# Graph attention on one Trainium2 core: the weighted sum over neighbours with the features as the loaded operand

## The chip, the cores and the metric

One core of a Trainium2 chip runs the whole program. The metric is the device time of one execution in microseconds; three runs of the kernel before were timed.

## The reference, cut to what matters

Four graphs of 256 nodes go through two graph attention layers (8 heads of 32 outputs) and then through a transformer block with a mixture of experts. The change touches the graph layers alone:

```python
def gat_layer(x, adj, W, a_self, a_neigh, b):
    feat = jnp.einsum('nf,hfo->hno', x, W)
    attn_self = jnp.einsum('hno,ho->hn', feat, a_self)
    attn_neigh = jnp.einsum('hno,ho->hn', feat, a_neigh)
    e = attn_self[:, :, None] + attn_neigh[:, None, :]
    e = jax.nn.leaky_relu(e, LRELU_ALPHA)
    e = e + MASK_VAL * (1.0 - adj)[None, :, :]
    alpha = jax.nn.softmax(e, axis=-1)
    out = jnp.einsum('hnm,hmo->hno', alpha, feat) + b[:, None, :]
    out = jnp.transpose(out, (1, 0, 2)).reshape(out.shape[1], -1)
    return jax.nn.elu(out)
...
x = x + _L0_xattn_ref(ctx_512, _layernorm(x, axis=-1), ...)
x = x + _L0_ffn_ref(_layernorm(x, axis=-1), ...)
```

## The kernel before, in words

Each engine runs its own hand-written program; semaphores join them. The work of one graph is cut into 48 steps, and tables of steps (`UNIT_AT`, `TRANS_LAG`, `PV_LAG`, `OUT_AT`, `QKV_AT`, ...) say which piece stands in which step. First the graph layers of graph 0 run alone (the part ahead of the loop). Then a loop of three passes runs, in each step, the graph layers of graph b + 1 (`gat(b + 1, s)`) and behind them the pieces of the transformer block of graph b. Last comes the block of graph 3 alone. On every engine the order within a step is fixed: the graph layer's instructions first, then the block's.

A graph layer has 8 units: two halves of the rows (t = 0, 1, 128 rows each) times four pairs of heads. For a unit, TensorE makes the scores of two heads (`zb`, L424), ScalarE copies them (L625), VectorE does the leaky ReLU and the mask (L895, L904), GpSimd shifts (L735), TensorE transposes four 128x128 blocks into the bank `tb` (L432), ScalarE takes the exponential of that bank into `gpT` (L630), and TensorE multiplies with the features (L443). The transposes of unit k stand 4 steps behind its scores, the product 5 steps: so in one step TensorE transposes unit k + 1 and then multiplies unit k.

The product of a unit is 4 calls. A call loads a 128x128 block of the attention weights and streams 33 columns of `feat`: the 32 features of a head and a column of ones, so that the sum of the weights, by which the result is divided, comes out as column 33. The result stands in `ob` with the rows of the graph on the partitions. After the four units of a half, in the step `done(l, t)`, VectorE divides (L911, L913) and adds the bias (L916); one step later (`ELU_LAG`) ScalarE (L634) and VectorE (L920, L921) do the ELU. In step `OUT_AT` (20) TensorE transposes layer 0's output (L455), which starts layer 1. `ob`, `tb` and `zb` are single banks: the next writer waits until the last reader is through (`o_free`, `t_free`, `z_free`).

Of the kernel before, what the change touches and what calls it, by code (L numbers as in the profile page):

```python
# [12 lines left out]
P = 128  # L13
# [5 lines left out]
FE = FO + 1  # L19
# [63 lines left out]
ELU_LAG = 1  # L83
# [56 lines left out]

def summed(s):

    return [n for n, at in enumerate(SUM_AT) if at == s]
# [17 lines left out]
def block_program(nc, x, ctxT, w0, w1, gat_rows, norm_cols, qk_rows, wqkv, wo, wgate, wgu, wd, consts, spread, out):  # L161
    ctx = ExitStack()
    with ctx:
        def sb(name, shape, dt=F32):
            return ctx.enter_context(nc.sbuf_tensor(name, shape, dt))
# [4 lines left out]
        def sem(name):  # L170
            return ctx.enter_context(nc.semaphore(name))
# [11 lines left out]
        qkw = sb("qkw", [P, 2 * HD])  # L183
# [27 lines left out]
        gsum = sb("gsum", [P, H])  # L211
        go = rows[:, 2 * D:4 * D].rearrange("p (t d) -> p t d", t=T)
# [3 lines left out]
        hid = sb("hid", [P, T, D])  # L216
        hn = gex
# [64 lines left out]
        pv_done, o_free = sem("pv_done"), sem("o_free")  # L282
        gout_ready, gexp_ready, gres_ready, hn_ready = sem("gout_ready"), sem("gexp_ready"), sem("gres_ready"), sem("hn_ready")
# [18 lines left out]
        def t_value(b, l, n):  # L302


            return b * 2 * (NU + 3) + l * (NU + 3) + n + 1
# [39 lines left out]
        def _(sp):  # L345
# [9 lines left out]
            sp.dma_start(qkw[:, :], qk_rows).then_inc(in_gat, 16)  # L355
# [30 lines left out]
        def _(pe):  # L386
            def gat(b, a):

                for l in range(2):
# [45 lines left out]
                    for k in units(l, a - PV_LAG):  # L435
                        t, hp = divmod(k, H // 2)
                        pe.wait_ge(t_free, t_value(b, l, k + 2) + 1)
                        if hp == 0:
                            pe.wait_ge(o_free, b * 2 * T + l * T + t + 1)
                        for h in range(2):  # L440
                            hh = 2 * hp + h
                            for m in range(T):
                                mm = pe.matmul(ob[:, hh * FE:(hh + 1) * FE], gpT[:, k % 3, h, m, :], feat[:, m, hh, :],  # L443
                                               start=(m == 0), stop=(m == T - 1))
                        mm.then_inc(pv_done, 1)
                if a in (OUT_AT, HN_AT):
# [161 lines left out]
        def _(act):  # L608
            def gat(b, a):
                for l in range(2):  # L610
# [20 lines left out]
                    for t in range(T):  # L631
                        if a == done(l, t) + ELU_LAG:
                            act.wait_ge(gout_ready, b * 2 * T + l * T + t + 1)
                            act.activation(gex[:, t, :], go[:, t, :], ACT.Exp).then_inc(gexp_ready, 1)  # L634
# [181 lines left out]
        def _(dve):  # L816
# [37 lines left out]
            def gat(b, a):  # L854
# [18 lines left out]
                for l in range(2):  # L873
# [33 lines left out]
                    for t in range(T):  # L907
                        if a == done(l, t):
                            dve.wait_ge(pv_done, unit(b, l, 4 * t + 4))
                            o_ = ob[:, 0:H * FE].rearrange("p (h o) -> p h o", h=H)  # L910
# [3 lines left out]
                               .then_inc(o_free, 1)  # L914
                            dve.wait_ge(o_free, b * 2 * T + l * T + t + 2)
# [241 lines left out]
            for t in range(T):  # L1157
                link(dve.memset(feat[:, t, :, FO:FE], 1.0))

            dve.sem_inc(z_free, 1)  # L1160
            dve.sem_inc(t_free, 1)
            dve.sem_inc(o_free, 1)
# [73 lines left out]
```

## Time and profile before

| | |
|---|---|
| median of 3 timed runs | 677.07 us (676.18 to 681.5) |
| span of the profiled execution | 676.1 us |
| TensorE matmul busy | 604.8 us, 89% of the span |
| TensorE weight load busy | 445.9 us, 66% |
| VectorE busy | 441.0 us, 65% |
| ScalarE busy | 266.7 us, 39% |
| GpSimd busy | 292.0 us, 43% |
| mean granted TensorE clock | 0.944 |

The profile gives each instruction's start and duration on the chip. A matmul's duration holds its way through the array, so the pace of matmuls is read from start to start. PE is TensorE's matmul, PEld its weight load, DVE is VectorE, ACT is ScalarE, POOL is GpSimd. The granted clock is 1.00 at the full level and 0.50 at the lower. The part ahead of the loop ends near 100 us, the passes of the loop end near 250, 403 and 557 us, and the last block fills the rest.

### The profile page before, as it was taken

Reading aid. Unit: us, or ns where it says so; the run is one execution under the profiler, and the core shown is the slowest. Engines: PE = TensorE matmul, PEld = TensorE weight load, DVE = VectorE, ACT = ScalarE, POOL = GpSimd, SP = SyncE. Lnnn points to the kernel's source line nnn. Section 1 sums busy time; section 2 is a strip of 40 time slices with the busy share of each in tenths; the row PEclk is TensorE's granted clock in tenths of the full one; section 3 lists DMA queues with packets and bytes.
Section 4 is the critical chain, followed back from the end, with each engine's and each line's share of the span. In section 5 each row is a group of like instructions: output and inputs, shape, how many; then the busy total and the mean of one; then the engine's idle time right before and its main releaser. Section 6 shows DMA issues by size and latency. Waiting matters only on the chain.

```text
span 676.1 us, 11574 instructions
## 1 busy us (share of the span) xinstructions
PE 604.8 (89%) x3140; PEld 445.9 (66%) x3140; DVE 441.0 (65%) x1277; ACT 266.7 (39%) x653; POOL 292.0 (43%) x588
## 2 busy tenths in 40 slices
PE   2786938979999998879999998879999998999998
PEld 1573933559678873558778973458777974676786
DVE  5727537975738756985738765986738766565363
ACT  2313305546533304636633304647633303674020
POOL 1514325885424023886425023886424126773000
PEclk9997558898999998979999998989999999999999
DMA  8900000000000000000000000000000000000000
GB/s 313 380 6 0 2 16 4 1 2 1 0 1 2 2 26 10 4 0 2 0 1 1 1 26 10 1 0 1 1 1 1 1 1 16 1 1 1 1 1 16
DMA packets 8305, 14.51 MB, mean 21 GB/s; under 512 B 860, under 2 KB 7068, under 8 KB 7988
## 3 DMA queue, kind: packets, MB, share of 16 engines
q1 hardware_dynamic: 8244, 13.76, 5.8%
q8 instruction: 31, 0.51, 0.3%
q14 instruction: 30, 0.25, 0.1%
HBM read 12.70 MB, written 1.05 MB: 20 GB/s over the span
## 4 chain that ended last, share of the span: by engine, by line
PE 56%; DVE 16%; issue 13%; POOL 9%; ACT 4%; POOLq 1%; DMA 1%; DVEq 0%; ACTq 0%; SPq 0%
PE bank L565 10%; PE bank L463 9%; PE ob L443 9%; PE bank L523 5%; PE tb L432 5%; PE bank L542 4%; DVE tt L904 3%; POOL m L775 2%; PE bank L538 2%; PE bank L534 2%; PE bank L509 2%; DVE lr L895 2%; PE zb L424 1%; ACT prob L666 1%; PE zb L414 1%
## 5 line engine op out<-in xcount | busy, mean ns | idle before, releaser
L735 POOL TENSOR_SCALAR tt<-tt,gmn 128x256 f32<-128x256 f32 x128 | 77.1, 613 | 64.1 <-DVE gmn L904 63.5
L509 PE MATMUL bank<-wqkv_sb,hT 128*128 128x512 f32 x192 | 97.9, 648 | 0.0
L666 ACT ACTIVATE prob<-bank,sneg,rms 128x128 f32<-128x128 f32 (+1 forms) x128 | 64.0, 507 | 68.5 <-DVE sneg L995 67.7
L775 POOL TENSOR_TENSOR m<-early,rope_s 128x256 f32<-128x256 f32 x80 | 70.8, 908 | 42.1 <-ACT early L647 41.8
L463 PE MATMUL bank<-m,wgu_sb 128*128 128x128 f32 (+1 forms) x480 | 86.6, 330 | 1.0 <-DVE m L1025 0.6
L791 POOL TENSOR_SCALAR prob<-prob,srcp 128x128 f32<-128x128 f32 (+1 forms) x128 | 53.7, 436 | 55.5 <-DVE srcp L1066 55.4
L463 PEld LDWEIGHTS bank<-m,wgu_sb 128*128 128x128 f32 x480 | 71.2, 191 | 9.2 <-issue 2.2
L443 PEld LDWEIGHTS ob<-feat,gpT 128*128 128x128 f32 x512 | 75.8, 227 | 0.8 <-issue 0.6
L443 PE MATMUL ob<-feat,gpT 128*128 128x33 f32 x512 | 75.2, 297 | 0.0
L895 DVE SCALAR_TENSOR_TENSOR lr<-zs 128x512 f32<-128x512 f32 x64 | 50.9, 797 | 25.3 <-ACT zs L625 22.6
L904 DVE CUSTOM_DVE_ANT_0 tt<-lr,maskv 128x256 f32<-128x256 f32 x128 | 62.3, 522 | 3.5 <-issue 2.9
L523 PE MATMUL bank<-kT,qT 128*128 128x128 f32 (+1 forms) x256 | 62.3, 360 | 0.9 <-ACT prob L666 0.9
L625 ACT ACTIVATE zs<-zb 128x512 f32<-128x512 f32 x64 | 38.3, 599 | 59.7 <-PE zb L424 56.5
L509 PEld LDWEIGHTS bank<-wqkv_sb,hT 128*128 128x128 f32 x192 | 36.3, 203 | 38.0 <-issue 35.0
L565 PE MATMUL bank<-wo_sb,qT 128*128 128x256 f32 x256 | 59.7, 383 | 0.3 <-ACT qT L672 0.3
L647 ACT ACTIVATE early<-bank 128x512 f32<-128x512 f32 x40 | 24.1, 603 | 89.8 <-PE bank L509 89.8
L565 PEld LDWEIGHTS bank<-wo_sb,qT 128*128 128x128 f32 x256 | 47.3, 190 | 10.0 <-issue 4.5
L432 PE MATMUL tb<-cst,tt 128*128 128x128 f32 x256 | 48.8, 322 | 4.6 <-ACT gpT L630 3.8
L523 PEld LDWEIGHTS bank<-kT,qT 128*128 128x128 f32 x256 | 41.4, 199 | 12.4 <-issue 6.3
L994 DVE TENSOR_REDUCE smx<-bank 128x2 f32<-128x512 f32 (+1 forms) x48 | 33.0, 686 | 24.8 <-PE bank L525 21.8
L630 ACT ACTIVATE gpT<-tb 128x512 f32<-128x512 f32 x64 | 38.4, 599 | 20.4 <-PE tb L432 19.9
L432 PEld LDWEIGHTS tb<-cst,tt 128*128 128x128 f32 x256 | 34.5, 169 | 17.1 <-issue 7.6
(151 smaller groups left out, 1026.5 us busy)
## 6 DMA issues: line engine op xcount, KB each, us to landing
wqkv_sb<-wqkv_dram SPq DMA_DIRECT2D x1, 3072.0 KB, 12.4
wgu_sb<-wgu_dram SPq DMA_DIRECT2D x2, 1408.0 KB, 11.2
wo_sb<-wo_dram SPq DMA_DIRECT2D x1, 2048.0 KB, 17.8
wd_sb<-wd_dram SPq DMA_DIRECT2D x1, 1408.0 KB, 15.6
xin<-x_dram SPq DMA_DIRECT2D x4, 256.0 KB, 2.7
out_dram<-rows SPq DMA_DIRECT2D x8, 128.0 KB, 1.9
rows<-gat_rows_dram SPq DMA_DIRECT2D x1, 512.0 KB
cst<-consts_dram SPq DMA_DIRECT2D x1, 425.0 KB, 3.6
```

What stands on the lines that cost most here:

```text
L432: mm = pe.transpose(tb[:, (h * T + m) * P:(h * T + m + 1) * P], tt[:, k % 3, h, m * P:(m + 1) * P], ident)
L443: mm = pe.matmul(ob[:, hh * FE:(hh + 1) * FE], gpT[:, k % 3, h, m, :], feat[:, m, hh, :], start=(m == 0), stop=(m == T - 1))
L463: mm = pe.matmul(ps[:, m * N + c0:m * N + c1], wgu_sb[:, m, k, n * P:(n + 1) * P], tokT[:, k, c0:c1], start=(k == 0), stop=(k == KT - 1))
L509: mm = pe.matmul(ps[:, :], hT[:, k, t * P:(t + 1) * P], wqkv_sb[:, k, c * G * HD:(c + 1) * G * HD], start=(k == 0), stop=(k == KT - 1))
L523: pe.matmul(ps[:, i * nk:(i + 1) * nk], qT[:, G * g + h, t * P:(t + 1) * P], kT[:, g, 0:nk], start=True, stop=False)
L565: mm = pe.matmul(bank_of(w)[:, 0:D], lhs[:, k, t * P:(t + 1) * P], rhs[:, k, :], start=(k == 0), stop=(k == end - 1))
L666: ins = act.activation(prob[:, n % 5, i * nk:(i + 1) * nk], ps[:, i * nk:(i + 1) * nk], ACT.Exp, bias=sneg[:, n, i:i + 1], scale=rq(g, t, ...
L735: ins = pool.tensor_scalar(tt[:, k % 3, h, :], tt[:, k % 3, h, :], -1.0, gmn[:, k % 3, h:h + 1], ALU.mult, ALU.add)
L775: ins = pool.tensor_tensor(dst[:, :, c, :], src[:, :, 1 - c, :], s_, ALU.mult)
L791: ins = pool.tensor_scalar(part_, part_, srcp[:, n, i:i + 1], 1.0, ALU.mult, ALU.mult)
L895: dve.scalar_tensor_tensor(lr[:, k % 2, :], zs[:, k % 2, :], 0.2, zs[:, k % 2, :], ALU.mult, ALU.min)\
L904: ins = dve.tensor_tensor_reduce(tt[:, k % 3, h, :], lr[:, k % 2, h * N:(h + 1) * N], maskv[:, t, :], 1.0, 3e38, ALU.add, ALU.min, gmn[:, ...
```

## The change

The two operands of the product change places. `feat` gets 64 columns per head (32 features, a column of ones, 31 zeros); the 64 columns of one head are the loaded operand, and a 128x128 block of the transposed attention weights streams, 128 columns. The two heads of a unit go to the two column halves of the array: head 0 writes partitions 0 to 63 of `ob`, head 1 partitions 64 to 127. So the result stands turned: head and feature on the partitions, rows of the graph on the columns. When a half of the rows is done, ScalarE copies `ob` to the new tensor `goT`; one step later TensorE turns it back with four transposes into `tb`, and VectorE divides from there. The ELU moves one step on. The order in which `tb` is filled is now a computed list (`TURNED`). To make room, `qkw` lies in the memory of `hid`.

```diff
-FE = FO + 1
+FE = 2 * FO
...
-ELU_LAG = 1
+BACK_LAG, ELU_LAG = 1, 2
...
+def turned_fills():
+    order = []
+    for a in range(STEPS):
+        for l in range(2):
+            if a == TERMS_AT[l]:
+                order.append((l, 0))
+            if a == PARTS_AT[l]:
+                order.append((l, 1))
+            order += [(l, k + 2) for k in units(l, a - TRANS_LAG)]
+            order += [(l, "back", t) for t in range(T) if a == done(l, t) + BACK_LAG]
+        if a in (OUT_AT, HN_AT):
+            order.append((0 if a != HN_AT else 1, NU + 2))
+    return {fill: n for n, fill in enumerate(order)}
...
+        goT = sb("goT", [P, H // 2, P])
+        qkw = hid[:, 0, :]
...
                         pe.wait_ge(t_free, t_value(b, l, k + 2) + 1)
-                        if hp == 0:
-                            pe.wait_ge(o_free, b * 2 * T + l * T + t + 1)
-                        for h in range(2):
-                            hh = 2 * hp + h
-                            for m in range(T):
-                                mm = pe.matmul(ob[:, hh * FE:(hh + 1) * FE], gpT[:, k % 3, h, m, :], feat[:, m, hh, :],
-                                               start=(m == 0), stop=(m == T - 1))
+                        if hp == 0 and (t or l or not isinstance(b, int)):
+                            pe.wait_ge(goT_ready, b * 2 * T + l * T + t)
+                        for m in range(T):
+                            for h in range(2):
+                                mm = pe.matmul(ob[h * FE:(h + 1) * FE, hp * P:(hp + 1) * P], feat[:, m, 2 * hp + h, :],
+                                               gpT[:, k % 3, h, m, :], start=(m == 0), stop=(m == T - 1))
                         mm.then_inc(pv_done, 1)
+                    for t in range(T):
+                        if a == done(l, t) + BACK_LAG:
+                            pe.wait_ge(goT_ready, b * 2 * T + l * T + t + 1)
+                            pe.wait_ge(t_free, back_value(b, l, t))
+                            pe.nop(nofuse=True)
+                            for hp in range(H // 2):
+                                mm = pe.transpose(tb[:, hp * P:(hp + 1) * P], goT[:, hp, :], ident)
+                            mm.then_inc(t_full, 1)
...
+                        if a == done(l, t):
+                            act.wait_ge(pv_done, unit(b, l, 4 * t + 4))
+                            if t or l or not isinstance(b, int):
+                                act.wait_ge(gout_ready, b * 2 * T + l * T + t)
+                            act.activation(goT[:, :, :].rearrange("p h q -> p (h q)"), ob[:, :], ACT.Copy).then_inc(goT_ready, 1)
...
-                        if a == done(l, t):
-                            dve.wait_ge(pv_done, unit(b, l, 4 * t + 4))
-                            o_ = ob[:, 0:H * FE].rearrange("p (h o) -> p h o", h=H)
+                        if a == done(l, t) + BACK_LAG:
+                            dve.wait_ge(t_full, back_value(b, l, t))
+                            o_ = tb[:, :].rearrange("p (h o) -> p h o", h=H)
                             link_a(b, dve.reciprocal(gsum[:, :], o_[:, :, FO]))
...
-                link(dve.memset(feat[:, t, :, FO:FE], 1.0))
+                link(dve.memset(feat[:, t, :, FO:FE], 0.0))
+                link(dve.memset(feat[:, t, :, FO:FO + 1], 1.0))
```

Line numbers shift with it: L432 becomes L456, L443 becomes L466, and the transposes back are L475; ScalarE's copy is L667; VectorE's division L947 and L949.

On TensorE in the loop, layer 0, the step behind the first half's last product. Before, the four transposes of a unit into `tb`, the product of the unit before it into `ob`, and then the block's own transposes of `m`:

```order
L432 MATMUL tb<-cst,tt 128x128 x4
L439 REGISTER_ALU
L443 MATMUL ob<-feat,gpT 128x33 x4
L477 REGISTER_ALU
L517 MATMUL bank<-cst,m 128x128
L518 MATMUL bank<-cst,m 128x128
```

Of the change, with the transposes back of `goT` into the same bank:

```order
L456 MATMUL tb<-cst,tt 128x128 x4
L463 REGISTER_ALU
L466 MATMUL ob<-gpT,feat 64x128 x4
L472 REGISTER_ALU
L475 MATMUL tb<-cst,goT 128x128 x4
L508 REGISTER_ALU
L548 MATMUL bank<-cst,m 128x128
L549 MATMUL bank<-cst,m 128x128
```

The four transposes back stand between the product and the block's work, and write the bank that the unit's transposes of the same step have just filled; the exponential has to empty it first.

On ScalarE at the same place: the exponentials of two units (`gpT`), between them the block's copy (`qT`) and four softmax rows (`prob`). Before:

```order
L630 ACTIVATE gpT<-tb 128x512
L319 REGISTER_ALU
L656 ACTIVATE qT<-bank 128x4x128
L662 REGISTER_ALU
L666 ACTIVATE prob,ssum<-bank,sneg,rms 128x128 x4
L627 REGISTER_ALU
L630 ACTIVATE gpT<-tb 128x512
```

Of the change:

```order
L661 ACTIVATE gpT<-tb 128x512
L666 REGISTER_ALU
L667 ACTIVATE goT<-ob 128x512
L343 REGISTER_ALU
L692 ACTIVATE qT<-bank 128x4x128
L698 REGISTER_ALU
L702 ACTIVATE prob,ssum<-bank,sneg,rms 128x128 x4
L658 REGISTER_ALU
L661 ACTIVATE gpT<-tb 128x512
```

The copy of `ob` has come in behind the first exponential; the second, which empties `tb` for the transposes back, stays behind the softmax rows.

On TensorE ahead of the loop, the last units of layer 0 and the transposes of the layer's output (`gex`). Before:

```order
L432 MATMUL tb<-cst,tt 128x128 x4
L443 MATMUL ob<-feat,gpT 128x33 x4
L432 MATMUL tb<-cst,tt 128x128 x4
L443 MATMUL ob<-feat,gpT 128x33 x8
L455 MATMUL tb<-cst,gex 128x128 x4
```

Of the change:

```order
L475 MATMUL tb<-cst,goT 128x128 x4
L456 MATMUL tb<-cst,tt 128x128 x4
L466 MATMUL ob<-gpT,feat 64x128 x4
L456 MATMUL tb<-cst,tt 128x128 x4
L466 MATMUL ob<-gpT,feat 64x128 x8
L475 MATMUL tb<-cst,goT 128x128 x4
L486 MATMUL tb<-cst,gex 128x128 x4
```

Both turns stand alone between the layer's own instructions here; no block work lies beside them.

## Rows read from the trace of the kernel before

**Rows 1.** The page's head: the span.

```profile
span 676.1 us, 11574 instructions
```

**Rows 2.** The page's costliest groups, the product: records | busy us, mean ns | idle before.

```profile
L443 PE MATMUL ob<-feat,gpT 128*128 128x33 f32 x512 | 75.2, 297 | 0.0
```

**Rows 3.** Stretches: us, busy us (records) of PE, PEld, DVE, ACT, POOL, granted clock, DMA.

```profile
64.00:90.00 26.00, 22.94 (x100) 20.18 (x100) 13.78 (x45) 8.17 (x15) 10.02 (x16) 0.50 0.01 2
...
294.00:298.00 4.00, 0.06 (x1) 0.09 (x2) 1.63 (x2) 4.00 (x13) 4.00 (x6) 0.76 0.00 0
298.00:304.00 6.00, 6.00 (x28) 4.59 (x29) 5.86 (x13) 1.86 (x4) 4.89 (x9) 0.59 0.00 0
304.00:325.00 21.00, 20.65 (x155) 17.40 (x155) 13.15 (x41) 15.17 (x48) 12.72 (x33) 1.00 0.01 2
```

**Rows 4.** TensorE in order of time, layer 1 in the loop: start us, us, instruction.

```profile
371.28 0.98 PE L443 MATMUL ob<-feat,gpT 128*128 128x33 f32 x8
372.10 1.14 PE L463 MATMUL bank<-m,wgu_sb 128*128 128x128 f32 x8
373.07 0.60 PE L432 MATMUL tb<-cst,tt 128*128 128x128 f32 x4
373.51 0.98 PE L443 MATMUL ob<-feat,gpT 128*128 128x33 f32 x8
```

**Rows 5.** TensorE in order of time, around smaller array shapes.

```profile
281.95 0.27 PE L518 MATMUL bank<-cst,m 128*128 128x128 f32 x1
282.16 0.39 PE L424 MATMUL zb<-pair_r,pair_l 48*128 48x512 bf16 x1
282.47 0.66 PE L432 MATMUL tb<-cst,tt 128*128 128x128 f32 x4
...
315.37 0.22 PE L525 MATMUL bank<-causal,identb 128*128 128x128 bf16 x1
315.42 0.65 PE L523 MATMUL bank<-kT,qT 128*128 128x256 f32 x2
...
339.25 0.29 PE L408 MATMUL tb<-identb,parts 128*48 128x128 bf16 x2
339.47 1.99 PE L414 MATMUL zb<-w1x,hT 128*128 128x256 f32 x8
```

**Rows 6.** TensorE and ScalarE in order of time, layer 0 in the loop, units 4 and 5.

```profile
309.19 0.59 ACT L630 ACTIVATE gpT<-tb 128x512 f32<-128x512 f32 x1
...
309.85 0.65 PE L432 MATMUL tb<-cst,tt 128*128 128x128 f32 x4
...
311.14 0.46 ACT L666 ACTIVATE prob<-bank,sneg,rms 128x128 f32<-128x128 f32 x1 [0.87 <-DVE sneg L995]
...
312.90 0.60 ACT L630 ACTIVATE gpT<-tb 128x512 f32<-128x512 f32 x1
```

**Rows 7.** The end of layer 0 in the loop.

```profile
324.41 0.59 PE L523 MATMUL bank<-kT,qT 128*128 128x256 f32 x2
...
328.42 0.59 ACT L672 ACTIVATE qT<-bank 128x512 f32<-128x512 f32 x1
...
328.46 0.60 PE L455 MATMUL tb<-cst,gex 128*128 128x128 f32 x4
```

**Rows 8.** Ahead of the loop, the end of layer 0.

```profile
41.47 1.09 PE L432 MATMUL tb<-cst,tt 128*128 128x128 f32 x4
42.36 3.46 PE L443 MATMUL ob<-feat,gpT 128*128 128x33 f32 x16
...
45.86 0.21 DVE L911 RECIPROCAL gsum<-ob 128x8 f32<-128x8 f32 x1 [6.76 <-PE ob L443]
46.10 0.42 DVE L913 TENSOR_TENSOR rows<-ob,gsum 128x256 f32<-128x256 f32 x1
...
48.28 1.12 PE L455 MATMUL tb<-cst,gex 128*128 128x128 f32 x4 [2.46 <-DVE gex L921]
49.43 0.69 DVE L934 COPY hT<-tb 128x512 f32<-128x512 f32 x1 [1.21 <-PE tb L455]
```

More of the change, by code:

```diff
@@ L138, in done @@
     return UNIT_AT[l][NU // T * (t + 1) - 1] + PV_LAG
+def turned_fills():
[11 more added lines that the diff above has]
+    return {fill: n for n, fill in enumerate(order)}
+TURNED = turned_fills()
 def summed(s):
@@ L182, in block_program @@
         cols = sb("cols", [P, 2 * KT])
-        qkw = sb("qkw", [P, 2 * HD])
         rope_c = sb("rope_c", [P, 2, T, HD])
@@ L281, in block_program @@
         lrelu_done, score_ready, shifted = sem("lrelu_done"), sem("score_ready"), sem("shifted")
-        pv_done, o_free = sem("pv_done"), sem("o_free")
-        gout_ready, gexp_ready, gres_ready, hn_ready = sem("gout_ready"), sem("gexp_ready"), sem("gres_ready"), sem("hn_ready")
+        pv_done = sem("pv_done")
+        goT_ready, gout_ready, gexp_ready, gres_ready, hn_ready = sem("goT_ready"), sem("gout_ready"), sem("gexp_ready"), sem("gres_ready"), sem("hn_ready")
         ln_seed, pool_a, ln_ready, hid_ready = sem("ln_seed"), sem("pool_a"), sem("ln_ready"), sem("hid_ready")
@@ L302, in t_value, with back_value @@
         def t_value(b, l, n):
-            return b * 2 * (NU + 3) + l * (NU + 3) + n + 1
+            return b * len(TURNED) + TURNED[l, n] + 1
+        def back_value(b, l, t):
+            return b * len(TURNED) + TURNED[l, "back", t] + 1
         def unit(b, l, k):
@@ L354, in _ @@
             sp.dma_start(cols[:, :], norm_cols).then_inc(in_gat, 16)
-            sp.dma_start(qkw[:, :], qk_rows).then_inc(in_gat, 16)
+            sp.dma_start(qkw, qk_rows).then_inc(in_gat, 16)
             sp.dma_start(wqkv_sb[:, :, :], wqkv.rearrange("(k p) n -> p k n", p=P)).then_inc(in_qkv, 16)
@@ L913, in gat @@
                             dve.tensor_tensor(g_, o_[:, :, 0:FO], gsum[:, :].unsqueeze(2).broadcast_to([P, H, FO]), ALU.mult)\
-                               .then_inc(o_free, 1)
-                            dve.wait_ge(o_free, b * 2 * T + l * T + t + 2)
+                               .then_inc(t_free, 1)
+                            dve.wait_ge(t_free, back_value(b, l, t) + 1)
                             dve.tensor_tensor(go[:, t, :], go[:, t, :], rows[:, (4 + l) * D:(5 + l) * D], ALU.add)\
@@ L1157, in _ @@
             for t in range(T):
-                link(dve.memset(feat[:, t, :, FO:FE], 1.0))
+                link(dve.memset(feat[:, t, :, FO:FE], 0.0))
+                link(dve.memset(feat[:, t, :, FO:FO + 1], 1.0))
             dve.sem_inc(z_free, 1)
             dve.sem_inc(t_free, 1)
-            dve.sem_inc(o_free, 1)
             dve.sem_inc(lrelu_done, 2)
```

## The prediction

> **What bounds the kernel now.** The span of the profiled execution is 676.1 us [rows 1]; the three timed runs have a median of 677.07 us, so about 1 us lies around the span, and the sum below is made on the span and carried to the median.
>
> I read the table by stretch first, for the granted clock and for who is busy [rows 3]. The reader is to see three kinds of stretch. From 64 to 90 us, graph layer 1 of the first graph (it runs alone, ahead of the loop), TensorE is busy 22.94 of 26 us at a granted clock of 0.50, its lower level (1.2 GHz). From 304 to 325 us, in the second pass of the loop, it is busy 20.65 of 21 us at 1.00. And between 294 and 298 us it stood nearly still, after which the clock was 0.59 until 304 us. So after about 298 us of a pass, TensorE time is the time of the pass, and in the part ahead of the loop TensorE time at the low clock is. A saving or a cost in the product counts almost one to one there; only the first two of the 16 units of a pass (the first follows the transposes at 282.47 [rows 5]) lie before the idle stretch and are hidden by it.
>
> Then the product itself. Its group has 512 matmul records [rows 2], for 4 calls in each of 64 units, that is 256 calls: every f32 call is two passes, each with its own load of 128 columns. Eight passes stand from 371.28 to 372.10 us, 0.82 us or 0.102 each, though each streams only 33 columns; eight passes of the expert product, with 128 streamed columns, take 0.97 us (372.10 to 373.07), 0.12 each; four transposes of 128 columns take 0.44 us (373.07 to 373.51), 0.11 each [rows 4]. So with 33 columns the load sets the pace, and with 128 the stream is as long as the load was. At the low clock sixteen passes take 3.46 us with the last pass's tail, about 0.194 each in pitch and 1.55 for a unit, and four transposes 0.89 (41.47 to 42.36) [rows 8].
>
> **The change part by part.**
>
> *The swapped product.* A unit keeps its 4 calls and 8 passes. The load shrinks from 128 columns to 64, the stream grows from 33 to 128. One after the other, 8 passes at 0.11 are 0.88 us: no gain. A gain needs the two column halves to stream beside each other. No row shows that, so I bound it: 8 slots at worst, 4 at best. Within one half the two passes of a call follow each other in program order (half 0 twice, half 1 twice, again so), and if passes start in that order only the second pass of one half can lie beside the first of the other. That is 5 slots, 5 x 0.107 = 0.53 us, and I take it.
>
> *Changing the array's shape.* The unit now runs between transposes and products that use all 128 columns. Rows show what entering and leaving a smaller shape costs. The 48-row score matmul starts at 282.16, 0.21 us after a transpose at 281.95, where transposes follow each other by 0.11 [rows 4]: entering costs 0.10. Two bf16 transposes onto 48 columns, which hold the array in a 64-column shape, go from 339.25 to 339.47, 0.22 us, while a bf16 matmul of 128 columns in the full shape is followed after 0.05 (315.37 to 315.42) [rows 5]: leaving costs 0.22 - 0.10 = 0.12 with the last pass's tail. I take 0.10 each way, 0.20 per unit. The unit becomes 0.53 + 0.20 = 0.73 us against 0.82, so -0.08 us (bounds: 0.63 with 4 slots, 1.08 with 8). At the low clock: 5 x 0.213 + 0.20 = 1.27 against 1.55, -0.28 (bounds 1.05 and 1.90).
> The Trainium skill (TensorEngine Tiling (Array Packing), When to Use Tiling) recommends this very swap for a streamed side of up to 64 columns, and its Theoretical Speedup promises up to 2x for two tiles; by it alone a unit would be 0.41 us and the passes of the loop 14 x 0.41 = 5.7 us shorter. No row here shows two tiles at once, and rows 5 show the price of the shape, so the sum does not use it.
>
> *Turning back, in a pass of the loop.* Four times (two layers, two halves of the rows) ScalarE copies the bank (0.6 us by its 512-column exponentials [rows 6]), TensorE does 4 transposes (0.44 us [rows 4]), and VectorE reads the other bank. The transposes add 4 x 0.44 = 1.76 us on TensorE. Three waits come with them:
> - Layer 0, first half. The transposes into the shared bank now stand behind the exponential of unit 5 in the same step; before, that exponential was needed one step later. ScalarE runs behind: unit 5 is transposed at 309.85 and, with 0.44 for the transposes and 0.73 for unit 4's product, TensorE could turn back near 311.1, but its exponential starts only at 312.90, behind four softmax rows from 311.14 that had waited 0.87 us for VectorE [rows 6]. VectorE loses its division there (some 1.05 us), so that wait goes, while ScalarE gains a copy (about 0.5 in pitch); I put the exponential 0.4 earlier, at 312.5, its end at 313.1: TensorE waits 2.0 us. Queued behind it are the projections and scores of the step, all of which the pass needs.
> - Layer 0, second half. ELU moves one step later, while the step that transposes the layer's output stays. From the back transposes (where the score product at 324.41 stands now) to that step (328.46) are 4.05 us plus their own 0.44 [rows 7]; VectorE must divide, reduce a score, ScalarE do two softmax rows and the copy at 328.42, then the ELU exponential, then VectorE two ELU steps: about 5.3 us. TensorE waits 0.8.
> - Layer 1. ScalarE is close behind TensorE there, and I count 0.1.
> Together 1.76 + 2.0 + 0.8 + 0.1 = 4.7 us. Against this 14 units x 0.08 = 1.1 us. A pass costs 3.6 us more, three passes 10.8.
> If ScalarE is not behind when it matters, the three waits are nothing (1.8 instead of 4.7); if each is twice what I read, 7.6. I keep the reading.
>
> *Ahead of the loop.* 16 units x -0.28 = -4.5 us. Nothing covers the turning there. First half of a layer: 0.89 for the transposes, and then the next transposes wait until VectorE has read the bank: release 1.15 us after the start of four transposes (48.28 to 49.43), 0.21 + 0.42 of division and some 0.1 between, so about 1.0 more than the transposes themselves. Second half: the copy (0.60 + 0.1) and the transposes (1.15) stand between the last product and the division at 45.86 [rows 8]. That is 1.9 + 1.85 = 3.75 per layer, 7.5 for two. Sum +3.0 us.
>
> *The rest.* The memory of the norm rows shares space with a tensor that is written only after their last read; the added zeros and the dropped semaphore are a few short VectorE instructions in the setup. I take nothing: the setup is behind input loads. The reads of division change bank, not size.
>
> Sum: 10.8 + 3.0 = +13.8 us, 676.1 to 689.9; on the median 690.9 us, say 691. A measurement of this kernel tells about 1% from no change (the three runs reach from 676.18 to 681.5).
>
> **The rivals.**
>
> *The low clock goes away ahead of the loop (675.5 us, not slower).* The place is the two stretches of 8 units each, where about 22 of the 22.94 busy microseconds [rows 3] are theirs. The engine was busy but mostly loading there at 0.50; with 128 streamed columns it does more of what stretches at 1.00 do. After the idle at 294 us the clock came back by 304 us under dense streaming [rows 3]. For it: the swap lengthens the streams fourfold. Against: half of the array is idle in a lone half, and I cannot read what it takes. At the full clock 8 units take 8 x (0.44 + 0.73) + 4 x 0.31 = 10.6 us instead of 22, -11.4; letting the first 5 us of 22 stay low, -8.8; the turning then costs about 2.6 (1.3 for each half, with 0.44 for the transposes). So -6.2 per layer, -12.4 for two, against +10.8 in the loop: -1.6. It decides when the clock reads 1.00 in more than a half of each stretch.
>
> *The halves don't run beside each other (715 us).* Then a unit is 1.08 in the loop (+0.26 x 14 + 4.7 = 8.3 a pass, 25 in all) and 1.90 ahead of it (+0.35 x 16 + 7.5 = 13): +38 us. For it: nothing in this trace shows two matmuls at once. Against: the two halves write different partitions and share no column.
>
> *The swap does all it can (662 us, faster).* Four slots, no visible price of the shape, ScalarE in time: a unit 0.43, so -0.39 x 14 + 1.8 = -3.7 a pass, -11 in all; ahead of the loop 0.85 for 1.55, -11 + 7.5 = -3.5. Sum -14.5. Against: rows 5 and 6.
>
> **How the numbers follow.** Forecast 0.40, low clock gone 0.25, no halves side by side 0.20, all it can 0.15. The forecast's own range is 682 to 700 (the turning at 1.8 and 7.6 a pass). The whole range goes from 666 (half of the fastest case left out) to 712 (half of the slowest left out). Faster by over 1% is the fastest case and the lower edge of the clock's case, 0.20; within 1% most of the clock's case and the edge of the forecast, 0.22; slower the rest, 0.58.
>
> **What would show it.** Starts of the eight passes of a unit: 0.53 us from first to last plus a gap of 0.1 on either side is right; even steps of 0.11 mean no halves at once, pairs starting together mean four slots. TensorE should show an idle near 2 us ahead of the first back transposes of layer 0 in each pass, released by the exponential, and one under 1 us ahead of the layer's output transposes. The stretch of layer 1 ahead of the loop should keep its 0.50; a 1.00 there makes the forecast wrong, and so does a pass that is not 3 to 4 us longer than before.

## The result and the profile after

The changed kernel takes 684.41 us (median of 20 runs, 681.57 to 688.94) against 679.9 us for the kernel before (20 runs, 676.18 to 684.87): the ratio is 1.008, with a 95% interval of 1.0058 to 1.0101. The forecast was 691.0 against 677.07, 2% slower. The profiled execution after, the shortest of its 20, has a span of 679.8 us against 676.1 [rows 1]. The parts below are taken from these two executions.

Where the difference arises is read from one event that both programs have: the transposes of layer 1's output, with which the part ahead of the loop and each pass of the loop end. The timeline of TensorE in the kernel before:

```profile
97.16 1.12 PE L455 MATMUL tb<-cst,gex 128*128 128x128 f32 x4 [9.49 <-DVE gex L945]
249.53 0.60 PE L455 MATMUL tb<-cst,gex 128*128 128x128 f32 x4
402.99 0.60 PE L455 MATMUL tb<-cst,gex 128*128 128x128 f32 x4
556.40 0.60 PE L455 MATMUL tb<-cst,gex 128*128 128x128 f32 x4
```

And in the changed kernel:

```profile
88.58 1.12 PE L486 MATMUL tb<-cst,gex 128*128 128x128 f32 x4 [9.51 <-DVE gex L981]
245.32 0.60 PE L486 MATMUL tb<-cst,gex 128*128 128x128 f32 x4
402.93 0.60 PE L486 MATMUL tb<-cst,gex 128*128 128x128 f32 x4
561.76 0.60 PE L486 MATMUL tb<-cst,gex 128*128 128x128 f32 x4
```

The differences between these starts, and between the last one and the span:

| part | before, us | after, us | difference | forecast |
|---|---|---|---|---|
| ahead of the loop | 97.16 | 88.58 | -8.58 | +3.0 |
| pass 1 | 152.37 | 156.74 | +4.37 | +3.6 |
| pass 2 | 153.46 | 157.61 | +4.15 | +3.6 |
| pass 3 | 153.41 | 158.83 | +5.42 | +3.6 |
| last block | 119.7 | 118.0 | -1.7 | 0 |
| span | 676.1 | 679.8 | +3.7 | +13.8 |

So the loop lost 13.9 us where 10.8 were forecast, and the part ahead of the loop, where a loss was forecast, gained 8.6 us. The last block has the same code in both, and in other traces it takes 119.7 us (experiment 3) or 117.9 (experiment 4), so its -1.7 us says nothing of the change. Passes scatter too: with the loop's code unchanged they average 153.08 us here and 154.35 in experiment 5.

The stretch of layer 1 ahead of the loop, by the table of stretches (columns as in [rows 3]); in the kernel before the same stretch had TensorE busy for 22.94 us at a clock of 0.50 [rows 3]:

```profile
64.00:90.00 26.00, 13.77 (x106) 8.80 (x104) 13.68 (x46) 7.28 (x13) 12.56 (x26) 0.76 0.04 12
```

The timeline of TensorE shows the clock change between two instructions, in layer 0 (the first two lines) and in that stretch:

```profile
32.05 1.12 PE L466 MATMUL ob<-gpT,feat 128*64 128x128 f32 x8
...
34.13 0.66 PE L466 MATMUL ob<-gpT,feat 128*64 128x128 f32 x8
...
67.25 1.09 PE L466 MATMUL ob<-gpT,feat 128*64 128x128 f32 x8
68.27 0.39 PE L448 MATMUL zb<-pair_r,pair_l 48*128 48x512 bf16 x1
68.59 0.66 PE L456 MATMUL tb<-cst,tt 128*128 128x128 f32 x4
69.17 0.66 PE L466 MATMUL ob<-gpT,feat 128*64 128x128 f32 x8
...
74.27 0.63 PE L456 MATMUL tb<-cst,tt 128*128 128x128 f32 x4 [0.85 <-DVE rows L949]
```

The reader is to see the product fall from 1.12 to 0.66 us, near 34 us in layer 0 and near 68 in layer 1, and the wait of 0.85 us at 74.27, for the division, that the prediction had for the first half of a layer. For layer 0 the pace of the instructions has to tell the level, since the view of the clock reads 1.00 there even in the kernel before, where four transposes take 1.09 us [rows 8], as they do at 0.50 in layer 1:

```profile
26.00:45.00 19.00, 19.00 (x89) 17.68 (x88) 7.55 (x26) 5.68 (x10) 6.16 (x12) 1.00 0.44 168
```

So the mean clock of 0.944 in the table of the kernel before counts that time as full speed.

The costliest group of the product, answering to [rows 2], fell from 75.2 to 44.5 busy us:

```profile
L466 PE MATMUL ob<-gpT,feat 128*64 128x128 f32 x512 | 44.5, 297 | 0.2
```

In the second pass, the wait ahead of the first back transposes, in the timeline of TensorE:

```profile
304.16 0.66 PE L456 MATMUL tb<-cst,tt 128*128 128x128 f32 x4
304.75 0.66 PE L466 MATMUL ob<-gpT,feat 128*64 128x128 f32 x8
307.74 1.09 PE L475 MATMUL tb<-cst,goT 128*128 128x128 f32 x4 [2.34 <-ACT gpT L661]
308.62 0.42 PE L548 MATMUL bank<-cst,m 128*128 128x128 f32 x1
308.83 0.42 PE L549 MATMUL bank<-cst,m 128*128 128x128 f32 x1
...
327.89 0.65 PE L486 MATMUL tb<-cst,gex 128*128 128x128 f32 x4 [0.85 <-DVE gex L957]
```

TensorE waits 2.34 us for the exponential (forecast 2.0), and 0.85 us ahead of the output transposes (forecast 0.8). Behind the first wait stands something that was not forecast: the back transposes take 1.09 us and those of `m` start 0.21 us apart, twice the 0.11 that they have a few microseconds earlier. The clock had fallen; it falls near this wait in all three passes of this trace. The table of stretches says the same of this place:

```profile
304.00:311.00 7.00, 4.66 (x31) 3.98 (x29) 2.04 (x6) 3.87 (x13) 3.06 (x8) 0.76 0.00 0
311.00:325.00 14.00, 14.00 (x99) 10.07 (x98) 9.09 (x25) 8.31 (x28) 5.62 (x14) 1.00 0.01 2
```

### The profile page after: what moved, and what is told of

It is laid out like the page before. It is cut to its first block, busy times and chain, and to the rows that moved or that the text cites. A ratio compares the mean times of both kernels' runs of the same rounds, so it can differ in the third digit from the quotient of the medians.

```text
span 679.8 us, 11764 instructions
## 1 busy us (share of the span) xinstructions
PE 590.6 (87%) x3204; PEld 409.3 (60%) x3204; DVE 441.8 (65%) x1279; ACT 276.0 (41%) x669; POOL 295.1 (43%) x588
## 4 chain that ended last, share of the span: by engine, by line
PE 50%; DVE 19%; issue 13%; POOL 9%; ACT 6%; POOLq 1%; DMA 1%; DVEq 1%; ACTq 0%; SPq 0%
PE bank L596 11%; PE bank L494 8%; PE bank L554 5%; PE tb L456 5%; PE bank L573 4%; PE ob L466 4%; DVE tt L940 3%; ACT prob L702 2%; POOL m L811 2%; DVE lr L931 2%; PE bank L569 2%; PE bank L565 2%; ACT gpT L661 2%; DVE smx L1030 1%; PE zb L448 1%
## 5 line engine op out<-in xcount | busy, mean ns | idle before, releaser
L771 POOL TENSOR_SCALAR tt<-tt,gmn 128x256 f32<-128x256 f32 x128 | 81.1, 646 | 54.5 <-DVE gmn L940 53.9
L540 PE MATMUL bank<-wqkv_sb,hT 128*128 128x512 f32 x192 | 93.8, 625 | 0.5 <-ACT v_sb L678 0.5
L554 PE MATMUL bank<-kT,qT 128*128 128x128 f32 (+1 forms) x256 | 63.9, 366 | 0.9 <-ACT prob L702 0.9
L540 PEld LDWEIGHTS bank<-wqkv_sb,hT 128*128 128x128 f32 x192 | 34.9, 195 | 37.4 <-issue 34.6
L456 PE MATMUL tb<-cst,tt 128*128 128x128 f32 x256 | 45.8, 306 | 6.6 <-ACT gpT L661 4.1
L466 PE MATMUL ob<-gpT,feat 128*64 128x128 f32 x512 | 44.5, 297 | 0.2
L548 PE MATMUL bank<-cst,m 128*128 128x128 f32 x128 | 33.2, 295 | 12.7 <-ACT early L684 12.7
L456 PEld LDWEIGHTS tb<-cst,tt 128*128 128x128 f32 x256 | 31.0, 154 | 21.0 <-issue 11.5
```

The costliest lines, as they stand in the source:

```text
L456: mm = pe.transpose(tb[:, (h * T + m) * P:(h * T + m + 1) * P], tt[:, k % 3, h, m * P:(m + 1) * P], ident)
L466: mm = pe.matmul(ob[h * FE:(h + 1) * FE, hp * P:(hp + 1) * P], feat[:, m, 2 * hp + h, :], gpT[:, k % 3, h, m, :], start=(m == 0), stop=(m ...
L540: mm = pe.matmul(ps[:, :], hT[:, k, t * P:(t + 1) * P], wqkv_sb[:, k, c * G * HD:(c + 1) * G * HD], start=(k == 0), stop=(k == KT - 1))
L554: pe.matmul(ps[:, i * nk:(i + 1) * nk], qT[:, G * g + h, t * P:(t + 1) * P], kT[:, g, 0:nk], start=True, stop=False)
L771: ins = pool.tensor_scalar(tt[:, k % 3, h, :], tt[:, k % 3, h, :], -1.0, gmn[:, k % 3, h:h + 1], ALU.mult, ALU.add)
```

## The experiments

Two questions are left by this: what brought the full clock ahead of the loop, and what the loop's loss is made of. In the expectations, "the changed kernel" is the one above. For its parts the same events are compared as in the table.

### 1. Longer streams alone (kernel before, 64 columns)

```diff
-FE = FO + 1
+FE = 2 * FO
...
-                link(dve.memset(feat[:, t, :, FO:FE], 1.0))
+                link(dve.memset(feat[:, t, :, FO:FE], 0.0))
+                link(dve.memset(feat[:, t, :, FO:FO + 1], 1.0))
```

> The kernel before, with the operands as they were and only the features widened from 33 to 64 columns (31 of them zeros), so that each pass streams 64 columns against a 128-column load, and nothing is turned back. Theory A (the longer stream is what brings the full clock ahead of the loop): the clock of the stretch 64 to 90 us leaves 0.50, the passes there go from 0.194 us towards 0.11, layer 0 and layer 1 end several us earlier (normalised transposes near 90 us instead of 97), and the kernel is 5 to 8 us faster than before, since in the loop the pace stays set by the 128-column load (0.10 to 0.11 us a pass). Theory B (it is the smaller load, or the stream reaching 128 columns, and 64 columns do not do): the stretch keeps 0.50 and the time stays within 2 us of before.

Measured: 679.0 us against 678.15, ratio 1.0007 (0.9978 to 1.0036). The stretch of layer 1 keeps its clock:

```profile
64.00:90.00 26.00, 23.57 (x101) 20.19 (x100) 13.77 (x44) 8.14 (x15) 10.75 (x16) 0.50 0.01 2
```

Theory B: 64 streamed columns, 31 of them zeros, against a load of 128 did not do it.

### 2. The full array, no halves (changed kernel)

```diff
-                        for m in range(T):
-                            for h in range(2):
-                                mm = pe.matmul(ob[h * FE:(h + 1) * FE, hp * P:(hp + 1) * P], feat[:, m, 2 * hp + h, :],
+                        for h in range(2):
+                            for m in range(T):
+                                mm = pe.matmul(ob[:, hp * P:(hp + 1) * P], feat[:, m, 2 * hp:2 * hp + 2, :].rearrange("p h o -> p (h o)"),
```

> The changed kernel with both heads' 128 feature columns as the loaded operand in every call, head after head into the same 128 partitions: 8 passes of 128 loaded and 128 streamed columns on the full array, no change of the array's shape. The first head's result is overwritten, so half of the weighted sums are left out of the output. It tells what the column halves bring. Theory A (the halves stream beside each other and the shape changes cost little, as the unit's 0.59 us from start to next transposes in the changed kernel suggests): a unit takes 8 x 0.12 = 0.97 us in place of 0.59, so 14 x 0.38 = 5 us more a pass and 15 to 20 us more in all, 695 to 700 us. Theory B (my 5 slots with 0.2 us for two shape changes was right and the saving lies elsewhere): the unit is 0.88, 8 us more in all. The clock ahead of the loop: if the 128-column stream brings it, it is again near 0.76 in the stretch of layer 1; if the smaller load brings it, it is 0.50 again and the time is about 8 us longer still.

Measured: 687.8 us, ratio 1.0155 (1.0105 to 1.0206), with a span of 685.0. Layer 1 ahead of the loop, and a unit in the loop:

```profile
64.00:90.00 26.00, 14.62 (x102) 12.65 (x102) 12.75 (x43) 7.20 (x13) 10.80 (x25) 0.83 0.05 12
```

```profile
365.74 0.65 PE L456 MATMUL tb<-cst,tt 128*128 128x128 f32 x4
366.24 1.06 PE L466 MATMUL ob<-gpT,feat 128*128 128x128 f32 x8
367.13 0.28 PE L494 MATMUL bank<-m,wgu_sb 128*128 128x128 f32 x1
```

The clock is up with full loads too, so the smaller load is not what brings it. The product takes 0.89 us here from its start to the next instruction. In the changed kernel a unit at a like place reads

```profile
361.43 0.66 PE L456 MATMUL tb<-cst,tt 128*128 128x128 f32 x4
362.01 0.66 PE L466 MATMUL ob<-gpT,feat 128*64 128x128 f32 x8
362.60 1.16 PE L494 MATMUL bank<-m,wgu_sb 128*128 128x128 f32 x8
```

that is 0.58 for the transposes and 0.59 for the product, 1.17 together, against 0.50 + 0.89 = 1.39. The halves save 0.22 us per unit, not the 0.38 that was expected: a pass takes 0.11 us and not 0.12, and the expectation left out that the full array has no change of shape to pay. The span grew by 5.2 us and not by 15 to 20. A pass of the loop, (565.40 - 89.34) / 3 = 158.69 us, is only 1.0 us longer than with the change, where 14 x 0.22 would be 3.1; the wait for the exponential is shorter here (2.03 us for 2.34), and the clock falls near it in one pass of the three.

### 3. No turning back (changed kernel)

```diff
-BACK_LAG, ELU_LAG = 1, 2
+BACK_LAG, ELU_LAG = 0, 1
...
-                            act.activation(goT[:, :, :].rearrange("p h q -> p (h q)"), ob[:, :], ACT.Copy).then_inc(goT_ready, 1)
...
-                                mm = pe.transpose(tb[:, hp * P:(hp + 1) * P], goT[:, hp, :], ident)
...
-                            o_ = tb[:, :].rearrange("p (h o) -> p h o", h=H)
-                            link_a(b, dve.reciprocal(gsum[:, :], o_[:, :, FO]))
+                            o_ = ob[:, :].rearrange("p (h o) -> p h o", h=H)
+                            link_a(b, dve.reciprocal(gsum[:, :], feat[:, t, :, FO]))
```

> The changed kernel without turning back: no copy by ScalarE, no transposes; VectorE works on the turned bank itself in the step where the kernel before did, with a reciprocal of a row of ones in place of the sums, so the output leaves out the division and the turn. Theory A (turning back costs what the changed trace shows: 4 x 0.44 us of transposes, 2.3 us of wait for the exponential and about 1.3 us of low clock behind it, 0.85 us ahead of the output transposes, a pass; and 2 to 2.5 us for each half of a layer ahead of the loop): three passes 6.2 us shorter each, 18 us, and 5 to 9 us ahead of the loop, so 653 to 658 us against 680. Theory B (what ScalarE and VectorE owe comes due elsewhere in the step, as in the kernel before): only the transposes and the output wait go, 2.6 us a pass, and 5 us ahead of the loop, so about 667 us.

Measured: 657.16 us, ratio 0.9679 (0.9637 to 0.9722). The ends of the parts:

```profile
83.48 1.11 PE L477 MATMUL tb<-cst,gex 128*128 128x128 f32 x4 [9.52 <-DVE gex L969]
...
539.62 0.60 PE L477 MATMUL tb<-cst,gex 128*128 128x128 f32 x4
```

A pass takes (539.62 - 83.48) / 3 = 152.05 us; before it was (556.40 - 97.16) / 3 = 153.08, and with the change (561.76 - 88.58) / 3 = 157.73. So in these traces the swap by itself gains 1.0 us a pass, which is within the scatter of passes (153.08 to 154.35), and the turning costs 5.7. Ahead of the loop the swap gains 97.16 - 83.48 = 13.7 us and the turning costs 88.58 - 83.48 = 5.1. Theory A holds.

Two things make these amounts rough. The traced run here is the longest of its four (661.12 us) and the one with the change the shortest of its 20; by the two ratios, 1.008 and 0.9679, the turning costs some 27 us in all (an estimate), where the traces have 22. And the full clock comes at another time in each trace: here some 10 us after the first transposes of either layer, with the change 10 us after them in layer 0 and 6.5 in layer 1.

### 4. Turning into another bank (changed kernel)

The bank `zb` of the scores is idle in the steps of the turning. It gets two more fills per layer, and the transposes back, the division and their waits move to it.

```diff
-            order += [(l, "back", t) for t in range(T) if a == done(l, t) + BACK_LAG]
...
-            return b * 2 * (NU + 1) + l * (NU + 1) + n + 1
+            return b * 2 * (NU + 1 + T) + l * (NU + 1 + T) + n + 1
...
-                            pe.wait_ge(t_free, back_value(b, l, t))
+                            pe.wait_ge(z_free, back_value(b, l, t))
...
-                                mm = pe.transpose(tb[:, hp * P:(hp + 1) * P], goT[:, hp, :], ident)
+                                mm = pe.transpose(zb[:, hp * P:(hp + 1) * P], goT[:, hp, :], ident)
```

> The changed kernel with the back transposes written into the score bank, which is idle in these steps, in place of the bank that the exponential has still to empty. Theory A (the exponential is what the back transposes wait for, and the clock falls because TensorE stands still there): the wait of 2.3 us in each pass and the slow stretch of 1.3 us behind it go, 3 to 3.6 us a pass, 9 to 11 us in all, plus about 1 us at each half of a layer ahead of the loop where the next unit no longer waits for the division: 666 to 670 us, faster than before. Theory B (the block's own wait for the same late ScalarE and VectorE comes due right behind): no more than 3 us in all, 676 to 678 us.

Measured: 668.9 us (four runs, 664.02 to 675.29), ratio 0.9893 (0.9823 to 0.9963), faster than the kernel before, by about 1%. The trace is of the shortest run. The same place in the second pass:

```profile
296.51 0.66 PE L465 MATMUL ob<-gpT,feat 128*64 128x128 f32 x8
297.10 0.66 PE L474 MATMUL zb<-cst,goT 128*128 128x128 f32 x4
297.59 0.27 PE L547 MATMUL bank<-cst,m 128*128 128x128 f32 x1
297.70 0.27 PE L548 MATMUL bank<-cst,m 128*128 128x128 f32 x1
```

The wait of 2.34 us is gone, and the transposes of `m` start 0.11 us apart: the low clock behind the wait went with the wait, in all three passes. The passes average (544.28 - 83.40) / 3 = 153.63 us by the same event, 4.1 less than with the change, and the part ahead of the loop is 5.2 us shorter, more than the 2 to 4 expected there. Not all of that is the bank's: the full clock came 5.5 us after the first transposes in either layer, earlier than with the change (10 and 6.5), which by half the time is worth about 3 us (an estimate). Theory A.

### 5 and 6. Wide streams without the swap (kernel before)

`featw` is `feat` with 95 zero columns behind it; a call streams `w` columns from the head's own on, and what it writes beyond its 33 is overwritten by the next heads.

```diff
-                                mm = pe.matmul(ob[:, hh * FE:(hh + 1) * FE], gpT[:, k % 3, h, m, :], feat[:, m, hh, :],
+                                w = P if isinstance(b, int) else FE
+                                c = (m * H + hh) * FE
+                                mm = pe.matmul(ob[:, hh * FE:hh * FE + w], gpT[:, k % 3, h, m, :], featw[:, c:c + w],
```

> The kernel before, operands as they were, nothing turned back; only ahead of the loop each pass streams 128 columns in place of 33 (the head's own 33 and what lies behind them, whose results the next heads overwrite). Theory A (in these kernels the 128-column stream brings the full clock, whatever is loaded): the stretch 64 to 84 us reads well above 0.50, the normalised transposes ahead of the loop come 12 to 14 us earlier than in the kernel before (near 84 us in place of 97), the loop's passes stay at 153 us, and the time is 12 to 14 us below before, about 665 us. Theory B (the turned layout or the half loads were needed for it): the stretch keeps 0.50, each unit there takes 1.7 us or more in place of 1.55, and the time is 2 to 5 us above before.

Measured: 667.88 us, ratio 0.9822 (0.9768 to 0.9876), and

```profile
64.00:84.00 20.00, 10.29 (x82) 9.37 (x81) 10.82 (x36) 5.60 (x10) 8.19 (x22) 0.84 0.05 15
64.00:90.00 26.00, 15.19 (x94) 12.19 (x93) 12.53 (x42) 5.60 (x10) 10.02 (x23) 0.76 0.04 12
```

The part ahead of the loop ends at 84.13 us, 13.0 earlier than before. Neither the half loads nor the turned layout are needed for the clock. With `w = P` in the loop too:

> As the wide streams ahead of the loop, but in the loop too. Theory A (a pass of 128 loaded and 128 streamed columns takes 0.11 to 0.12 us at the full clock against 0.10 with 33 columns): a unit in the loop grows by 0.07 us, 1 us a pass, 3 us more than with the wide streams ahead of the loop alone, about 668 us. Theory B (the longer stream also shortens the low clock behind the idle stretch of each pass): passes no longer than 153 us, the same time as with the wide streams ahead of the loop alone.

Measured: 663.93 us, ratio 0.9777 (0.9702 to 0.9852). Once more, in more rounds:

> The kernel with wide streams everywhere once more, in more rounds, since its interval was wide: if its first time holds, 662 to 667 us and a ratio of 0.975 to 0.985 to the kernel before; if the first time was luck with the low clock's spells, it comes near the 668 us of the version with wide streams ahead of the loop alone.

Measured: 664.94 us, ratio 0.9784 (0.9748 to 0.9821). Of the versions that leave nothing out it is the fastest, ahead of the kernel before and of the changed one. The 3 us that the wider streams should have cost in the loop do not show: its passes take (543.26 - 83.97) / 3 = 153.1 us, as before. By the single records of the traces a pass starts 0.112 us behind the pass ahead of it with 33 columns (the kernel before, 371.31 to 372.10 us) as with 128 (experiment 2); only the first step of a unit is shorter with 33, 0.03 us. Whether the low clock in the loop is shorter for it is not settled: the intervals of experiments 5 and 6 overlap.

### 7. The calls head by head (changed kernel)

```diff
-                        for m in range(T):
-                            for h in range(2):
+                        for h in range(2):
+                            for m in range(T):
```

> The changed kernel with the two loops of the product exchanged: both calls of head 0 first, then both of head 1, so neighbours in the queue are in the same column half. Theory A (a pass lies beside the pass ahead of it only if that one is in the other half, which made 5 slots of 8 passes): now only one pair can lie side by side, 7 slots, so the product's 0.59 us from its first start to the next transposes becomes about 0.80, 0.2 us more in 14 units of three passes and 16 units ahead of the loop, 10 to 12 us longer than the changed kernel. Theory B (a pass of half the columns is simply shorter, and nothing lies side by side): 0.59 stays and so does the time.

Measured: 686.13 us in the traced run; its second run took 1154.33 us, so no ratio is given. The product still takes 0.59 us to the next instruction. Its own instructions alone, in three short stretches (us, PE busy with the count in flight, clock, then share and GB/s of the DMA):

```profile
368.70:368.74 0.04, 0.03 (x2) 1.00 0.00 0
368.74:368.86 0.12, 0.12 (x2) 1.00 0.00 0
368.86:368.90 0.04, 0.04 (x4) 1.00 0.00 0
```

Theory A fell, and B is not right either: two passes start within 0.04 us, 0.12 us nothing starts, then two more. The same view of the changed kernel:

```profile
368.22:368.26 0.04, 0.02 (x2) 1.00 0.00 0
368.26:368.39 0.13, 0.13 (x2) 1.00 0.00 0
368.39:368.42 0.03, 0.03 (x4) 1.00 0.00 0
```

So passes start in pairs in either order of the calls. By the single records of the trace the starts of this unit in the changed kernel are 0, 0.007, 0.160, 0.167, 0.269, 0.276, 0.379 and 0.385 us, and the next instruction starts at 0.588.

### 8. Output transposes a step later (turning in the other bank)

```diff
-OUT_AT = 20
+OUT_AT = 21
```

> The turning back in the score bank as before, and besides layer 0's output transposes one step later (step 21 for 20), so that the ELU has the distance again that it had before the change. Theory A (the 0.85 us wait for the ELU in each pass is a plain loss): 0.8 us a pass, 2 to 2.5 us shorter than with the output transposes in step 20. Theory B (the next wait, of layer 1's first product for the copy that VectorE makes of this bank, comes due in its place, one step behind): no gain, or up to 2 us longer.

Measured: 671.16 us, ratio 0.9879 (0.983 to 0.9929). No gain: theory B in its verdict. The wait of the output transposes for the ELU is gone from the loop (2.5 us in one place is left in the table of waits, ahead of the loop), and TensorE's wait at L572 for VectorE's copies of `pT` stands there with 2.6 us. That these two are one and the same loss is not shown.

### 9. Both heads in one half (changed kernel)

```diff
-                        for m in range(T):
-                            for h in range(2):
-                                mm = pe.matmul(ob[h * FE:(h + 1) * FE, hp * P:(hp + 1) * P], feat[:, m, 2 * hp + h, :],
+                        for h in range(2):
+                            for m in range(T):
+                                mm = pe.matmul(ob[0:FE, hp * P:(hp + 1) * P], feat[:, m, 2 * hp + h, :],
...
+                    link(dve.memset(ob[:, :], 1.0))
```

> The changed kernel with both heads in the same column half: the second head's calls write partitions 0 to 63 too, over the first head's, so half of the weighted sums are left out (the other partitions hold ones from the setup). Theory A (two halves work side by side, four pairs 0.11 us apart in either order of the calls): with one half the passes follow each other, eight slots of 0.109, and the product takes 0.05 + 7 x 0.109 + 0.203 = 1.02 us from its first start to the next instruction in place of 0.59; 0.43 us more in each of 14 units of three passes and 16 units ahead of the loop, some 20 to 26 us more than the changed kernel. Theory B (a pass of 64 loaded columns is simply half as long): 0.59 stays and so does the time.

The calls stand head by head, as in experiment 7, which is the kernel to compare with. Measured: 706.11 us, ratio 1.0394 (1.0334 to 1.0454). A unit in the loop, and the counts at its start:

```profile
378.11 1.09 PE L466 MATMUL ob<-gpT,feat 128*64 128x128 f32 x8
379.13 0.44 PE L577 MATMUL bank<-cst,m 128*128 128x128 f32 x2
```

```profile
378.09:378.13 0.04, 0.02 (x1) 1.00 0.00 0
378.13:378.25 0.12, 0.12 (x1) 1.00 0.00 0
378.25:378.30 0.05, 0.05 (x2) 1.00 0.00 0
```

One pass at a time, and 1.02 us to the next instruction, the number that theory A gave. The pairs of experiment 7 are the two halves side by side. The Trainium skill (TensorEngine Tiling (Array Packing), Key Properties) says that tiles load and multiply independently of each other and that a change of the tiling mode drains the engine; these runs agree with the first, by 0.59 against 1.02 us, and the gaps priced below fit the second, though no record shows what fills them.

## Why the prediction was wrong, and where it was right

**The step that failed is "Ahead of the loop": the sum of +3.0 us at the low clock.** The stretch measured -8.6 us. What the first rival said came true instead: the full clock came in each of the two stretches of units, some 10 us into the 19 of layer 0 (a little under half of it is left, where the rival asked for more than a half) and 6.5 us into the 17 of layer 1. Its own terms were -17.6 us for the swap and +5.2 for the turning; experiment 3 gives -13.7 and +5.1. Of the 3.9 us that the swap fell short of that rival, 0.7 are the setup's (below). The clock more than covers the rest: the rival let it stay low for 5 us of a layer, and in experiment 3 it stayed low for some 10; by the rival's own 22 us at the low clock and 10.6 at the full one, 5 us more cost about 2.6 a layer (an estimate). The +5.1 meets its +5.2 in part by luck, since the clock did not come at the same time in the two traces. Put -8.6 in place of +3.0 and the sum is +2.2 us, against +3.7 in the profile; the loop's 13.9 for 10.8 and the last block's -1.7 make the difference. The prediction had named the longer stream and gave it 0.25; of the clock with half of the array idle it said "I cannot read what it takes". Rows of before alone could not tell it; experiments 1, 2, 3 and 5 do. All are the stretch of 64 to 90 us, which holds the first microseconds of the units at the low clock and, in the faster kernels, idle time behind them, so that only 0.50 against more is to be read from it:

| kernel | loaded x streamed columns | turned back | clock |
|---|---|---|---|
| before | 128 x 33 | no | 0.50 |
| experiment 1 | 128 x 64 | no | 0.50 |
| experiment 5 | 128 x 128 | no | 0.76 |
| experiment 2 | 128 x 128 | yes | 0.83 |
| experiment 3 | 64 x 128 | no | 0.70 |
| changed | 64 x 128 | yes | 0.76 |

Experiments 1 and 5 load the same operand and differ in the stream, in its length and also in what it holds: 31 of the 64 columns of experiment 1 are zeros, while the added columns of experiment 5 are mostly the next heads' features. Which of the two counts was not tried apart. TensorE was busy for 22.94 and 23.57 of 26 us in the first two rows, and yet the clock stayed at its lower level (1.2 GHz). How the chip decides was not tried.

**The unit of the product: -0.13 us against -0.08, with two errors of opposite sign.** The forecast had five slots of 0.107 and 0.20 for the change of shape. From the start of the last transpose to the next instruction behind the product, the single records of the trace give 0.92 us before and 0.79 after. The passes run in four slots of 0.109, not five: the order in the program, from which the five came, does not decide (experiment 7). The shape costs more than 0.20: from the last transpose to the first half pass is 0.203, from the last half pass to the next instruction again 0.203, 0.094 above a slot each, and the first slot is 0.160, 0.051 too long; together 0.24 us. So the slots were put 0.10 us too long and the shape 0.04 too short. Experiment 3, where nothing else of the change is left in the loop, has 1.0 us gained a pass. The forecast was 14 x 0.08 = 1.1, but 14 x 0.13 would be 1.8, and the scatter of passes is 1.3: that 1.0 and 1.1 meet is luck. The reading that the load sets the pace with 33 columns, at 0.102 us, and the stream with 128, at 0.12, was also off: both are 0.112 from pass to pass, and the rest was the first step of each group.

**Turning back in a pass: 5.7 us against 4.7.** The step "Layer 0, first half" had the right wait (2.34 for 2.0) and its right cause, the shared bank behind a late exponential: with the other bank it goes (experiment 4). What it missed is the clock that falls near such a wait: of the 4.1 us that experiment 4 gives back per pass, the wait is 2.3 and the transposes of `m` and the turning at half speed most of the rest, (1.09 - 0.66) + 8 x 0.10 = 1.2 us at that one place. The fall is not certain: in experiment 7 the same wait of 2.33 us in the second pass, up to 313.18 us, is followed by eight transposes of `m` 0.11 us apart, the full pace. "Layer 0, second half" was right (0.85 for 0.8). Without that wait nothing was gained, though (experiment 8).

**The rest: +0.7 us instead of nothing (part of the -8.6).** TensorE's first wait, for the setup's semaphore, was 7.8 us before and 8.5 after, in the table of waits:

```profile
PE tb L400 <- DVEq L1169: 7.8, 1, 7.8
```

```profile
PE tb L424 <- DVEq L1205: 8.5, 1, 8.5
```

The setup was not hidden behind input loads; experiments 1 and 5, which fill more columns in it as well, have 8.7 there.

**The other rivals.** "The halves don't run beside each other" priced a unit at 1.08 and the kernel at 715 us; experiment 9, which makes it so, has 1.02 from the first start, 1.11 with the entry into the shape, and 706. "The swap does all it can" had its four slots, but neither its free shape nor its ScalarE in time.

## What to carry to other kernels

Where an engine is busy but its clock is low, look at what it is busy with: here 128-column streams in place of 33, with results that are thrown away, brought the clock back and 2% of the whole kernel, with no change to the data's layout. When work is inserted that writes a shared bank, ask who still has to empty that bank: the turning itself was cheap (1.6 us a pass with the idle bank, experiment 4 against 3), and what cost was its 2.3 us wait for a late exponential, with a low clock behind it in most passes; the idle bank took both away.

## What the runs showed of the hardware that was not expected

- Two column halves of 64 run their passes side by side, in pairs 0.01 us apart, whatever the order of the calls: 0.59 us for eight passes against 1.02 in one half (experiments 7 and 9). TensorE does not keep the program's order between the halves: head by head, the passes that start 0.014 us apart cannot be neighbours in the program, since neighbours in one half start 0.109 apart.
- At the full clock, a pass with 33 streamed columns and one with 128 cost the same on the full array, 0.112 us from start to start, both with 128 loaded columns; for eight it is 0.82 us against 0.89 ([rows 4] and experiment 2), by the first step.
- The full clock came at a different time in two executions of one kernel: in experiment 6 near 28 and 66 us, in its repeat near 30 and 64, by the pace of the instructions.
- A wait of 2.3 us in the loop was followed by 2.6 us at half speed (307.74 to 310.33 us in the trace after), and without the wait the same instructions ran at the full clock (experiment 4). With the wait the clock fell near it in three passes of three with the change and in one of three in experiment 2 (wait 2.03 us).
